# DLRM tower on one core: an unrolled, time-ordered rewriting with eleven one-hot lookups

## The chip, the cores and the metric

The kernel runs on one core of one Trainium2 chip. The metric is device time in microseconds of one execution, the median of the runs shown. TensorE (PE), VectorE (DVE), ScalarE (ACT) and GpSimd (POOL) each run their own instruction list in order; SyncE (SP) issues DMAs. They meet only at semaphores.

## The reference

```
e = stack([tbl_t[ids[:, t]] for t in 0..25], axis=1)       # 2048 x 26 x 128
combined = concat([dense[:, None, :], e], axis=1)          # 27 features of 128 numbers
inter = einsum('bfd,bgd->bfg', combined, combined)         # 27 x 27 per sample
z = concat([dense, inter[:, upper triangle]], axis=1)      # 128 + 351
h = relu(concat([z, dense]) @ W_top1 + b_top1)             # 607 -> 512
h = relu(h @ W_top2 + b_top2)                              # 512 -> 256
y = h @ W_top3                                             # 256 -> 1
```

Batch is 2048, everything float32. Twelve of the tables have 1000 rows, six 1250, seven 12500 and one 125000.

## The kernel before

The batch is cut in four blocks of 512 samples, each of four tiles of 128. The first three blocks run in a hardware loop (`Fori`), the last is written out once more. An embedding reaches PE's working tensor `emb` in one of two ways.

**Gathered** (17 tables). POOL issues one indirect DMA per table and tile (`gather`, L396), 272 in all, each fetching 128 rows. PE transposes them (`embed`, L416), and ACT copies the bank to `emb` (L535). `rows` has room for four tiles, so POOL runs a whole block ahead.

**Looked up** (9 of the 1000-row tables). The table is loaded anew for every block, ACT rounds it to float32r (`table_h`, L543), DVE subtracts to get the remainder (`table_l`, L640). DVE makes one-hot matrices: a `tensor_scalar` per 125-row chunk compares the ids, broadcast over partitions, with a per-partition row number, both operands in SBUF (L650). PE multiplies, two matmuls of 512 columns per chunk (L436, L438), 16 per lookup, and ACT copies the result to `emb` (L549, L558).

`emb` is laid out sample by sample: the 27 features of a sample lie side by side. A **gram** step (L454) is 64 small products, 26 x 26, one per sample; four samples' results go to four 32-partition strips of one PSUM bank. Each product shows as two weight loads and two matmuls in the trace. DVE copies each gram bank to SBUF (L663), turns 32 x 32 blocks (L670), and ACT and DVE collect the pairs row by row (L565, L677). PE transposes the pairs (L467), ACT and DVE split them in two parts (L574, L687), and the MLP runs in three matmuls per product: `layer1` (L485 to L488), `layer2` (L498 to L501), `layer3` (L511). ACT writes relu twice, once to SBUF in float32 (L586) and once as float32r (L588), and DVE takes the difference (L699).

The order on every engine comes from two written lists: `BODY` (grams of the block, embeds of its last two tiles, the first lookups of the next block) and `TAIL` (MLP of the block, mixed with the other lookups and first embeds of the next one). Grams stand mostly back to back in `BODY`. The PSUM banks are three for embeddings, three for grams and transposed pairs, two for the MLP.

Of the kernel before, what the change touches and what calls it, by code (L numbers as in the profile page):

```python
# [12 lines left out]
LOOKUPS = 9  # L33
LOOKED_UP = [t for t in range(TABLES) if VOCAB[t] == 1000][:LOOKUPS]
GATHERED = [t for t in range(TABLES) if t not in LOOKED_UP]

ORDER = [0] + [t + 1 for t in GATHERED] + [t + 1 for t in LOOKED_UP]


def pair_rows():  # L40

    rows = []
    for r in range(FEATURES):
        for s in range(r + 1, FEATURES):
            a, b = sorted((ORDER[r], ORDER[s]))
            rows.append(DIM + a * FEATURES - a * (a + 1) // 2 + (b - a - 1))
    return rows


def dlrm_tower(nc, dense, ids_gathered, ids_looked_up, tables, w1_dense, w1_pairs, b1, w2, b2, w3,  # L50
               out):
    fp32, fp32r = mybir.dt.float32, mybir.dt.float32r
    i32, u32 = mybir.dt.int32, mybir.dt.uint32
    ALU, ACT = mybir.AluOpType, mybir.ActivationFunctionType

    TILE, TILES = 128, 4
# [12 lines left out]
    KCH = [128, 128, PAIRS - 256, DIM]
    N1, N2 = HIDDEN1 // 128, HIDDEN2 // 128  # L70
    ONE_HOTS = 9
    assert LOOKUPS * CHUNKS % ONE_HOTS == 0

    EARLY = 2
    lookups = [("lookup", i, h) for i in range(LOOKUPS) for h in range(2)]  # L80
    early, halves = lookups[:2 * EARLY], lookups[2 * EARLY:]
    embeds = [("embed", t, e) for t in range(TILES - 2) for e in range(len(EMBED))]

    PARTS = ((3,), (0,), (1, 2))
    LAST = len(PARTS) - 1
    own = [[("layer1", 0, 0)], [("layer1", 1, 0), ("z", 0, 0), ("z", 1, 0), ("z", 2, 0)],
           [("z", 0, 1), ("z", 1, 1)], [("z", 2, 1)],
           [("layer1", 0, 1)], [("layer1", 1, 1)], [("layer1", 0, 2)], [("layer1", 1, 2)],
           [("layer1", 2, p) for p in range(3)], [("layer1", 3, p) for p in range(3)], "E",
           [("layer2", 0)], [("layer2", 1)], "E", [("layer3",)], "E", "E", "E", "E", "E", "E"]  # L90
    TAIL = [("place", i) for i in range(EARLY)] + [("pair", 1)] + halves[:1]
    spaces = own.count("E")
    for k, steps in enumerate(own):
        if steps == "E":
            n = len(embeds) // spaces
            spaces, steps, embeds = spaces - 1, embeds[:n], embeds[n:]
        TAIL += steps

        upto = -(-(k + 1) * len(halves) // len(own))
        if "E" in own[k + 1:k + 2]:  # L100
            upto += upto % 2
        TAIL += [s for s in halves[:upto] if s not in TAIL]
    assert len(TAIL) == len(set(TAIL))
    tile2, tile3 = ([("embed", t, e) for e in range(len(EMBED))] for t in (2, 3))
    BODY = [("gram", 0), ("gram", 1), ("gram", 2), *tile2, ("gram", 3), ("gram", 4),
            *early, *tile3[:-1], ("dense",), ("gram", 5, 0), tile3[-1], ("gram", 5, 1),
            ("split", EARLY + 1), ("pair", 0), ("gram", 6), ("gram", 7)]

    EMB_USES = [s for s in TAIL + BODY if s[0] == "embed" or (s in halves and s[2] == 1)]
    MIX_USES = [("gram", n) for n in range(GRAMS)] + [("z", 0), ("z", 1), ("z", 2)] + [("none",)]

    MLP_USES = [("place", i) for i in range(EARLY)] + [("layer1", n) for n in range(N1)] + \
        [("layer2", n) for n in range(N2)] + [("layer3",), ("none",)]
    assert len(MLP_USES) % 2 == 0
    assert len(EMB_USES) % 3 == 0 and len(MIX_USES) % 3 == 0

    PAIR_TILES = [slice(0, TILES - 1), slice(TILES - 1, TILES)]
    PAIR_ACT = 11
    first_pair = [r * SIDE - r * (r - 1) // 2 for r in range(SIDE)]

    ctx = ExitStack()
    with ctx:
# [9 lines left out]
        emb = sb("emb", [128, BLOCK, FEATURES])  # L136


        shared_at = nc.sbuf_base
        shared = sb("shared", [128, 2 * N1 * BLOCK])  # L140
        gram = nc.alloc_sbuf_tensor_at("gram", [128, SIDE, 128], fp32, offset=shared_at)
        h1h = nc.alloc_sbuf_tensor_at("h1h", [128, N1, BLOCK], fp32r, offset=shared_at)
        h1l = nc.alloc_sbuf_tensor_at("h1l", [128, N1, BLOCK], fp32r, offset=shared_at + N1 * BLOCK * 4)
        rows = sb("rows", [128, TILES, NG, DIM])
        dense_rows = sb("dense_rows", [128, TILES, DIM])


        shared_z_at = nc.sbuf_base
        shared_z = sb("shared_z", [128, TILES * SIDE * 32])
        turned = nc.alloc_sbuf_tensor_at("turned", [128, TILES, SIDE, 32], u32, offset=shared_z_at)  # L150
        zh = nc.alloc_sbuf_tensor_at("zh", [128, 3, BLOCK], fp32r, offset=shared_z_at)
        zl = nc.alloc_sbuf_tensor_at("zl", [128, 3, BLOCK], fp32r, offset=shared_z_at + 3 * BLOCK * 4)
        dense_h = sb("dense_h", [128, BLOCK], fp32r)
        dense_l = sb("dense_l", [128, BLOCK], fp32r)
        pairs = sb("pairs", [128, 4, PAIRS])
        gather_ids = sb("gather_ids", [128, TILES, NG], i32)
        w1h = sb("w1h", [128, 4, HIDDEN1], fp32r)
# [30 lines left out]
        zeroed = sem("zeroed")
# [581 lines left out]
```

## Time and profile before

| | |
|---|---|
| median of 3 runs | 431.82 us (426.78 to 437.46) |
| profiled execution, span | 432.4 us |
| PE / weight loads busy | 330.4 / 266.8 us |
| DVE busy | 239.1 us |
| ACT busy | 179.4 us |
| POOL busy | 308.9 us |
| mean granted TensorE clock | 0.881 |
| DMA | 49.51 MB, 115 GB/s |

The profiled execution is one more execution, with its own span; the runs are others. POOL's busy time is the issuing of gathers. Matmul records overlap their neighbours, so the sum of a group's durations is more than the engine's time on it; the distance between two starts is the rate.

### The profile page before, as it was taken

Reading aid. Unit: us, or ns where it says so; the run is one execution under the profiler, and the core shown is the slowest. Engines: PE = TensorE matmul, PEld = TensorE weight load, DVE = VectorE, ACT = ScalarE, POOL = GpSimd, SP = SyncE. Lnnn points to the kernel's source line nnn. Section 1 sums busy time; section 2 is a strip of 40 time slices with the busy share of each in tenths; the row PEclk is TensorE's granted clock in tenths of the full one; section 3 lists DMA queues with packets and bytes.
Section 4 is the critical chain, followed back from the end, with each engine's and each line's share of the span. In section 5 each row is a group of like instructions: output and inputs, shape, how many; then the busy total and the mean of one; then the engine's idle time right before and its main releaser. Section 6 shows DMA issues by size and latency. Waiting matters only on the chain.

```text
span 432.4 us, 13310 instructions
## 1 busy us (share of the span) xinstructions
PE 330.4 (76%) x5360; PEld 266.8 (62%) x5360; DVE 239.1 (55%) x471; ACT 179.4 (41%) x363; POOL 308.9 (71%) x280
## 2 busy tenths in 40 slices
PE   0785719677699998286879999376969999867596
PEld 0563517466578876275668877264758887656475
DVE  2776625397569563266768664075666758023531
ACT  2144223720746546220546545420564546323442
POOL 6887878887778877777778878777777877772000
PEclk9899977888979999659969999666879999986699
DMA  5467853435435345426444543526354442221000
GB/s 155 153 177 191 239 167 109 128 92 151 115 110 149 118 122 117 133 52 167 119 130 114 158 116 106 141 55 169 77 172 100 142 123 71 55 57 28 5 0 0
DMA packets 24707, 49.51 MB, mean 115 GB/s; under 512 B 8010, under 2 KB 10586, under 8 KB 24653
## 3 DMA queue, kind: packets, MB, share of 16 engines
q1 hardware_dynamic: 15916, 30.83, 22.4%
q0 software_dynamic: 8704, 17.84, 17.5%
q8 instruction: 47, 0.77, 0.7%
q14 instruction: 8, 0.06, 0.0%
q10 hardware_dynamic: 32, 0.01, 0.0%
HBM read 48.65 MB, written 0.01 MB: 113 GB/s over the span
## 4 chain that ended last, share of the span: by engine, by line
PE 65%; issue 15%; DMA 10%; ACT 5%; DVE 3%; SPq 0%; ACTq 0%; DVEq 0%
PE mix_ps L454 12%; PE emb_ps L436 12%; PE emb_ps L438 11%; PE emb_ps L416 6%; DMA lookup_ids<-ids_looked_up 5%; DMA table<-table 5%; PE mlp_ps L485 4%; PE mlp_ps L488 4%; PE mlp_ps L486 4%; PE mlp_ps L436 3%; PE mlp_ps L438 3%; DVE one_hot L650 2%; ACT emb L535 2%; PE mlp_ps L498 2%; PE mlp_ps L501 2%
## 5 line engine op out<-in xcount | busy, mean ns | idle before, releaser
L396 POOL DMA_INDIRECT rows<-table,gather_ids x272 | 307.9, 1132 | 83.6 <-issue 81.7
L650 DVE TENSOR_SCALAR one_hot<-lookup_ids,row_number 125x512 fp32r<-125x512 int32 x288 | 124.8, 490 | 43.6 <-DMA lookup_ids<-ids_looked_up 17.6
L436 PE MATMUL emb_ps<-one_hot,table_h 125*128 125x512 f32 x224 | 94.2, 421 | 19.1 <-DVE table_l L640 18.7
L454 PE MATMUL mix_ps<-emb 128*26 128x26 f32 x4096 | 57.7, 202 | 54.3 <-issue 51.5
L438 PE MATMUL emb_ps<-one_hot,table_l 125*128 125x512 f32 x224 | 91.9, 410 | 0.0
L454 PEld LDWEIGHTS mix_ps<-emb 128*26 128x26 f32 x4096 | 49.5, 115 | 63.6 <-issue 61.7
L543 ACT ACTIVATE table_h<-table 125x1024 fp32r<-125x1024 f32 x36 | 38.0, 1060 | 88.9 <-DMA table<-table 52.4
L535 ACT ACTIVATE emb<-emb_ps 128x512 f32<-128x512 f32 (+1 forms) x80 | 46.9, 651 | 56.5 <-PE emb_ps L416 53.2
L663 DVE COPY gram<-mix_ps 128x416 f32<-128x416 f32 x32 | 27.8, 874 | 74.3 <-PE mix_ps L454 74.1
L436 PEld LDWEIGHTS emb_ps<-one_hot,table_h 125*128 125x128 f32 x224 | 44.6, 199 | 31.7 <-ACT emb L535 12.1
L549 ACT ACTIVATE emb<-emb_ps 128x512 f32<-128x512 f32 x28 | 34.0, 1215 | 50.2 <-PE emb_ps L438 50.1
L640 DVE TENSOR_TENSOR table_l<-table,table_h 125x1024 fp32r<-125x1024 f32 x36 | 43.6, 1212 | 13.6 <-ACT table_h L543 13.6
L438 PEld LDWEIGHTS emb_ps<-one_hot,table_l 125*128 125x128 f32 x224 | 44.7, 200 | 9.2
L436 PE MATMUL mlp_ps<-one_hot,table_h 125*128 125x512 f32 x64 | 31.0, 484 | 20.2 <-DVE one_hot L650 17.5
L416 PE MATMUL emb_ps<-ident,rows 128*128 128x128 f32 x272 | 42.7, 302 | 1.9 <-ACT emb L549 1.7
L416 PEld LDWEIGHTS emb_ps<-ident,rows 128*128 128x128 f32 x272 | 36.0, 158 | 6.9 <-ACT emb L549 1.9
L436 PEld LDWEIGHTS mlp_ps<-one_hot,table_h 125*128 125x128 f32 x64 | 15.0, 235 | 26.0 <-issue 15.0
L438 PE MATMUL mlp_ps<-one_hot,table_l 125*128 125x512 f32 x64 | 29.8, 466 | 0.0
L565 ACT ACTIVATE pairs<-turned 128x24 f32<-128x24 f32 (+33 forms) x148 | 19.0, 219 | 11.7 <-DVE turned L670 11.7
L699 DVE TENSOR_TENSOR h1l<-h_full,h1h 128x512 fp32r<-128x512 f32 x16 | 11.2, 700 | 22.0 <-ACT h1h L588 22.0
L586 ACT ACTIVATE h_full<-mlp_ps,b_sb 128x512 f32<-128x512 f32 x16 | 11.0, 689 | 20.7 <-PE mlp_ps L488 20.6
L485 PE MATMUL mlp_ps<-zh,w1h 128*128 128x512 f32 (+1 forms) x48 | 19.1, 398 | 0.5 <-ACT zh L574 0.5
(50 smaller groups left out, 278.4 us busy)
## 6 DMA issues: line engine op xcount, KB each, us to landing
table<-table SPq DMA_DIRECT2D x36, 500.0 KB
lookup_ids<-ids_looked_up SPq DMA_DIRECT2D x36, 256.0 KB, 5.4
rows<-table,gather_ids POOLq DMA_INDIRECT x272, 3.9
dense_rows<-dense SPq DMA_DIRECT2D x4, 256.0 KB, 4.1
gram<-w_pairs SPq DMA_DIRECT2D x2, 256.0 KB
gram<-w_dense SPq DMA_DIRECT2D x2, 256.0 KB
h_full<-w SPq DMA_DIRECT2D x1, 512.0 KB
gather_ids<-ids_gathered SPq DMA_DIRECT2D x16, 8.5 KB, 10.2
```

The costliest lines, as they stand in the source:

```text
L396: pool.indirect_dma_start(out=rows[:, t, g, :], out_offset=None, in_=tables[GATHERED[g]], in_offset=bass.IndirectOffsetOnAxis(ap=gather_id ...
L416: last = pe.transpose(bank[:, 128 * k:128 * k + 128], src, ident[:, :])
L436: pe.matmul(bank[:, :], table_h[0:TROWS, i % 2, cols], hot, start=(c == 0), stop=False)
L438: last = pe.matmul(bank[:, :], table_l[0:TROWS, i % 2, cols], hot, start=False, stop=(c == CHUNKS - 1))
L454: last = pe.matmul(bank[32 * j:32 * j + SIDE, SIDE * q:SIDE * q + SIDE], emb[:, s, 1:FEATURES], emb[:, s, 0:SIDE], start=True, stop=True)
L485: pe.matmul(mlp_bank(("layer1", n))[:, :], w1h[0:k, c, cols], high, start=(c == 3), stop=False)
L535: act.activation(emb[:, t * TILE:(t + 1) * TILE, EMBED[e][0]:EMBED[e][0] + k], emb_bank(("embed", t, e))[:, 0:128 * k].rearrange("p (k s) ...
L543: act.activation(table_h[0:TROWS, i % 2, :], table[0:TROWS, i % 2, :], ACT.Copy) \
L549: act.activation(emb[:, :, ROWED + i], emb_bank(("lookup", i, 1))[:, :], ACT.Copy) \
L640: dve.tensor_tensor(table_l[0:TROWS, i % 2, :], table[0:TROWS, i % 2, :], table_h[0:TROWS, i % 2, :].bitcast(fp32), ALU.subtract) \
L650: dve.tensor_scalar(one_hot[0:TROWS, hot_slot(i, c), :], lookup_ids[0:TROWS, i % 2, :], row_number[0:TROWS, c:c + 1], None, ALU.is_equal) \
L663: dve.tensor_copy(gram[:, :, HALF * n:HALF * n + HALF].rearrange("p r q -> p q r"), mix_bank(("gram", n))[:, 0:SIDE * HALF].rearrange("p ( ...
```

## The change

The kernel is written anew. There are no loops: every step has a time in units of a block, the steps are sorted by it once, and all engines walk that one list. What differs:

- Eleven tables are looked up and 15 gathered (240 gathers). `rows` holds two tiles instead of four, and a gather waits for the embed step two tiles back.
- Tables are padded to 1024 rows and split by ACT and DVE in the first two blocks only. In the second the split tables are also written to a DRAM scratch (1 MB each, 11 of them), and blocks three and four load them from there, without a split. Ids are int16.
- A one-hot step is a `tensor_tensor` over two chunks, 1024 elements per partition: ids in SBUF against row numbers in a PSUM bank, each operand repeated by a zero step. There are 176 instead of 288, and room for one lookup's.
- `emb` is laid out feature by feature. The copies that fill it write whole runs of 128; the gram matmuls read their 26 columns, as weights and as moving data, at a step of 128 elements.
- ACT, not DVE, copies the gram banks, two banks for them instead of three. Pairs are collected for two tiles at a time in ten ACT copies of bands.
- The MLP and the transposed pairs share two banks. Its first relu stays in PSUM and DVE subtracts from there. The last block's MLP is done as two units of two tiles.
- Each gram is two halves in the list, and a lookup half usually stands between.

```diff
-LOOKUPS = 9
+LOOKUPS = 11
...
+    def look_time(k, h):
+        b, i = divmod(k, LOOKUPS)
+        return b - 1 + (i + h / 2 + (0.3 if b > 0 else 0.0)) / LOOKUPS
+
+    for k in range(LOOKS):
+        at(look_time(k - 3, 1) if k >= 3 else -2.0 + k / 10, "load", k)
+        if k < SPLIT_BLOCKS * LOOKUPS:
+            at(look_time(k - 1, 0) - 0.001 if k >= 1 else -1.5, "split", k)
+        if SPLIT_BLOCKS - 1 == k // LOOKUPS and SPLIT_BLOCKS < BLOCKS:
+            at(look_time(k, 0) - 0.002, "spill", k)
+        for h in range(2):
+            at(look_time(k - 1, h) + 0.001 if k >= 1 else -1.4 + h / 10, "hots", k, h)
+            at(look_time(k, h), "look", k, h)
+    for t in range(TILES):
...
+        for e in range(EMBEDS):
+            at((t + 0.02 + 0.06 * e) / PER_BLOCK if t > 0 else (-0.6, -0.5, -0.4, -0.3)[e], "embed", t, e)
+        for n in (2 * t, 2 * t + 1):
+            for h in range(2):
+                at((t + 0.4 + 0.3 * (n % 2) + 0.14 * h) / PER_BLOCK, "gram", n, h)
...
-        emb = sb("emb", [128, BLOCK, FEATURES])
+        emb = sb("emb", [128, PLACES * WIDE - 1, TILE])
...
+            def load(k):
...
+                    sp.dma_start(table_hl[:, s, :, :].bitcast(fp32), scratch[i]).then_inc(hl_in[s], 16)
+                wait(sp, hot_ready, QUADS * (k - LIDS + 1))
...
+            def spill(k):
+                sp.wait_ge(table_low, k + 1)
+                sp.dma_start(scratch[k % LOOKUPS], table_hl[:, k % HL, :, :].bitcast(fp32)).then_inc(spilled[k % HL], 16)
...
+            for t in range(TILES):
...
+                for e in range(EMBEDS):
+                    wait(pool, embeds_done, EMBEDS * (t - ROWS) + e + 1)
...
-                        last = pe.matmul(bank[32 * j:32 * j + SIDE, SIDE * q:SIDE * q + SIDE],
-                                         emb[:, s, 1:FEATURES], emb[:, s, 0:SIDE], start=True, stop=True)
+                        last = pe.matmul(bank[32 * j:32 * j + SIDE, SIDE * q:SIDE * q + SIDE],
+                                         emb[:, f + 1:f + FEATURES, s], emb[:, f:f + SIDE, s], start=True, stop=True)
...
+                act.activation(gram_sb[:, t % 2, :, HALF * side:HALF * side + HALF].rearrange("p r q -> p q r"),
+                               mix_ps[n % 2][:, 0:SIDE * HALF].rearrange("p (q r) -> p q r", r=SIDE), ACT.Copy) \
+                    .then_inc(gram_out, 1)
...
-                    dve.tensor_scalar(one_hot[0:TROWS, hot_slot(i, c), :], lookup_ids[0:TROWS, i % 2, :],
-                                      row_number[0:TROWS, c:c + 1], None, ALU.is_equal) \
-                        .then_inc(hot_ready, 1)
+                for p in (2 * h, 2 * h + 1):
+                    wait(dve, hot_used, QUADS * (k - 1) + p + 1)
+                    dve.tensor_tensor(hot[:, p, :, :],
+                                      bass.AP(lids, k % LIDS * BLOCK, [[LIDS * BLOCK, 128], [0, 2], [1, BLOCK]]),
+                                      bass.AP(row_ps, 2 * p, [[CHUNKS, 128], [1, 2], [0, BLOCK]]),
+                                      ALU.is_equal).then_inc(hot_ready, 1)
```

## Rows read from the trace of the kernel before

**Rows 1.** The page, parts 1 and 4: busy time, and the chain that ended last.

```profile
PE 330.4 (76%) x5360; PEld 266.8 (62%) x5360; DVE 239.1 (55%) x471; ACT 179.4 (41%) x363; POOL 308.9 (71%) x280
PE 65%; issue 15%; DMA 10%; ACT 5%; DVE 3%; SPq 0%; ACTq 0%; DVEq 0%
```

**Rows 2.** The page, part 5: gathers; count, busy, mean ns, idle and its releaser.

```profile
L396 POOL DMA_INDIRECT rows<-table,gather_ids x272 | 307.9, 1132 | 83.6 <-issue 81.7
```

**Rows 3.** Windows of one loop turn: busy us of each engine, clock, DMA share.

```profile
171.60:270.80 99.20, 80.02 (x1340) 65.58 (x1340) 58.17 (x116) 43.75 (x91) 77.86 (x71) 0.88 0.45 123
```

**Rows 4.** Timeline, POOL beside DVE: start us, us, instruction, idle before it.

```profile
55.76 0.94 POOL L396 DMA_INDIRECT rows<-table,gather_ids  x1 [0.30 <-issue]
...
130.09 1.88 DVE L687 TENSOR_TENSOR zl<-mix_ps,zh 128x512 fp32r<-128x512 f32 x3 [1.48 <-ACT zh L574]
...
131.16 0.94 POOL L396 DMA_INDIRECT rows<-table,gather_ids  x1 [0.30 <-issue]
...
133.47 1.21 DVE L640 TENSOR_TENSOR table_l<-table,table_h 125x1024 fp32r<-125x1024 f32 x1
134.61 1.66 DVE L650 TENSOR_SCALAR one_hot<-lookup_ids,row_number 125x512 fp32r<-125x512 int32 x4
...
133.98 2.41 POOL L396 DMA_INDIRECT rows<-table,gather_ids  x1 [0.30 <-issue]
```

**Rows 5.** Timeline, PE at the full clock: first and last of 16 lookup matmuls; transposes.

```profile
155.51 0.40 PE L436 MATMUL emb_ps<-one_hot,table_h 125*128 125x512 f32 x1
...
158.94 0.39 PE L438 MATMUL emb_ps<-one_hot,table_l 125*128 125x512 f32 x1
...
54.42 1.04 PE L416 MATMUL emb_ps<-ident,rows 128*128 128x128 f32 x8
```

**Rows 6.** Timeline, PE in grams: one at the low clock, then the last ones.

```profile
179.76 2.03 PE L454 MATMUL mix_ps<-emb 128*26 128x26 f32 x127 [2.48 <-issue]
...
399.08 1.28 PE L454 MATMUL mix_ps<-emb 128*26 128x26 f32 x128 [0.42 <-issue]
402.90 1.28 PE L454 MATMUL mix_ps<-emb 128*26 128x26 f32 x128 [2.55 <-issue]
406.36 0.49 PE L454 MATMUL mix_ps<-emb 128*26 128x26 f32 x23 [2.17 <-issue]
```

**Rows 7.** The page, part 3: DMA queues, packets, MB, share of 16 engines.

```profile
q1 hardware_dynamic: 15916, 30.83, 22.4%
q0 software_dynamic: 8704, 17.84, 17.5%
q8 instruction: 47, 0.77, 0.7%
```

**Rows 8.** Groups by line, DVE and ACT: count, busy, mean ns, idle.

```profile
L650 DVE TENSOR_SCALAR one_hot<-lookup_ids,row_number 125x512 fp32r<-125x512 int32 x288 | 124.8, 490 | 43.6 <-DMA lookup_ids<-ids_looked_up 17.6 <-PE emb_ps L438 17.2 <-PE mlp_ps L438 8.6
L535 ACT ACTIVATE emb<-emb_ps 128x512 f32<-128x512 f32 (+1 forms) x80 | 46.9, 651 | 56.5 <-PE emb_ps L416 53.2 <-ACT y_rows L600 1.7 <-issue 1.4
L549 ACT ACTIVATE emb<-emb_ps 128x512 f32<-128x512 f32 x28 | 34.0, 1215 | 50.2 <-PE emb_ps L438 50.1
L588 ACT ACTIVATE h1h<-mlp_ps,b_sb 128x512 fp32r<-128x512 f32 x16 | 10.9, 681 | 0.0
L670 DVE STREAM_TRANSPOSE turned<-gram 128x832 uint32<-128x832 uint32 x16 | 16.7, 1045 | 0.5
```

**Rows 9.** Windows: the stretch in which the DMA engines are full.

```profile
40.00:50.00 10.00, 5.24 (x25) 3.84 (x23) 6.72 (x14) 3.87 (x5) 7.87 (x8) 1.00 1.00 263
```

**Rows 10.** Timeline: the first split and the last instruction.

```profile
10.08 1.22 DVE L640 TENSOR_TENSOR table_l<-table,table_h 125x1024 fp32r<-125x1024 f32 x1 [7.01 <-ACT table_h L543]
...
430.37 0.54 ACTq L604 DMA_DIRECT2D y<-y_rows  x1
```

More of the change, by code:

```diff
@@ L67, in dlrm_tower @@
+    WIDE = 14
+    PLACE = [1, 2, 3, 4, 5, 6, 7, 8, 1, 2, 3, 9, 4, 5, 6, 7]
+    PLACES = 10
     HALF = 16
-    GRAMS = TILE // 4 // HALF * TILES
     KCH = [128, 128, PAIRS - 256, DIM]
     N1, N2 = HIDDEN1 // 128, HIDDEN2 // 128
[L71 to L82, printed above, removed]
@@ L92, in dlrm_tower @@
[L92 to L104, printed above, removed]
@@ L105, in dlrm_tower @@
[L105 to L123, printed above, removed]
+    SPLIT_BLOCKS = 2
+    HL, RAW, LIDS, ROWS = 3, 3, 2, 2
+    LOOKS = BLOCKS * LOOKUPS
+    UNITS = [(0, 4), (4, 4), (8, 4), (12, 2), (14, 2)]
+    def unit_of(tile):
+        return [u for u, (t0, n) in enumerate(UNITS) if t0 <= tile < t0 + n][0]
@@ new lines, in features, with places @@
+        def features(tile):
+            return WIDE * (PLACES - 1 - PLACE[tile])
+        def places(b, f):
+            tiles = range(b * PER_BLOCK, (b + 1) * PER_BLOCK)
+            even = all(PLACE[t] == PLACE[t - 1] + 1 for t in tiles[1:])
+            for run in ([tiles] if even else [tiles[:-1], tiles[-1:]]):
+                first = (features(run[0]) + f) * TILE
+                pitch = (PLACES * WIDE - 1) * TILE
+                yield (slice((run[0] - tiles[0]) * TILE, (run[-1] + 1 - tiles[0]) * TILE),
+                       bass.AP(emb, first, [[pitch, 128], [-WIDE * TILE, len(run)], [1, TILE]]))
@@ L442, in grams @@
-            def grams(b, n, part=None):
-                if n % 2 == 0:
-                    need = [u for u in EMB_USES if u[0] == "lookup" or u[1] == n // 2]
-                    pe.wait_ge(emb_copied, emb_no(b, need[-1]) + 1)
-                if part != 1:
-                    pe.wait_ge(*mix_before(b, ("gram", n)))
-                bank = mix_bank(("gram", n))
-                for q in (range(HALF) if part is None else range(HALF)[part * HALF // 2:][:HALF // 2]):
+                    wait_emb_bank(pe, use)
@@ L742 @@
+            dve.tensor_copy(row_ps[:, :], row_number_i[:, :]).then_inc(rows_numbered, 1)
+            dve.wait_ge(rows_numbered, 1)
+            run({"split": split, "hots": hots, "embed": embed, "gram": gram, "z": z, "l1": l1, "weights": weights})
 def kernel(**inputs):
```

894 lines of the change are left out of this document (445 added, 449 removed).

## The prediction, made before the change was run

> **What bounds the kernel now.** I read busy times and the chain first. PE is busy for 76% of the span and makes up most of the chain, with 15% of it "issue"; POOL is busy for 71% [rows 1]. That points at PE, but the share is misleading. POOL's 272 gathers take 307.9 us busy and 83.6 us idle, of which 81.7 us is its own issuing: 391.5 us without a real wait, one gather per 1.44 us [rows 2]. One loop turn lasts 99.2 us and holds 68 gathers; 68 x 1.44 = 98 us, while PE is busy for 80 of the 99 [rows 3]. So POOL paces the loop, from 2.7 us to about 396, and 36 us of last block follow.
>
> A gather isn't slow by itself. With DVE idle it is 0.94 + 0.30 = 1.24 us. Beside DVE's subtraction from a PSUM bank it is the same 0.94. Under the split of a table (two SBUF inputs) and the one-hots (`tensor_scalar`, all in SBUF) one took 2.41 [rows 4]. Of the 391.5 us, 272 x 1.24 = 337 are gathers and 54 are DVE in their way.
>
> PE is close behind. A loop turn needs nine lookups of 16 x 0.229 = 3.66 us, 72 MLP matmuls at the same 0.23 us (16.6 us), and 84 transposes at 0.13 us (11 us) [rows 5]: 61 us. Then come eight grams. A gram's 128 matmuls run in 1.28 us at the full clock, but the next one starts 3.8 us after, with 2.55 us of "issue" between them [rows 6]. 256 instructions of 64 bytes are 16 KB, and the instruction queue brought 0.77 MB in 47 pieces, 16 KB each [rows 7]. I take it that grams back to back outrun the fetching of their instructions, one piece per 3.5 to 3.9 us: 8 x 3.9 = 31 us, in all 92 us per turn against POOL's 98.
>
> **The change, part by part.**
>
> *POOL.* 240 gathers x 1.24 = 298 us. The one-hots now have one input in PSUM, which is the form that left gathers alone [rows 4]. The 22 splits remain; the one under which a gather took 2.41 cost at most 1.5 us, so 0 to 33 us, taken 13. Per tile that is 18.7 us, and `rows` lets POOL start a tile when PE embeds the one two before. If PE needs 20 us or more per tile, as below, POOL waits for PE. It stops being the pace.
>
> *DVE.* A one-hot step is 1024 elements with two tensor inputs. The nearest row is the split, also 1024 elements and two inputs: 1.21 us, the next instruction starting 1.14 after it [rows 4]. Four per lookup are 4.6 us, where eight took 3.3 (1.66 us per four). With int16, the zero steps and PSUM unseen, bounds are 0.53 us (two elements per cycle, from the 512-element step at about 0.4) and 2.2 (the strided price below); I take 1.14, since the PSUM subtraction costs 1.88 / 3 = 0.63 us for 512, the same rate. A split adds 1.14.
>
> *PE.* 11 x 3.66 = 40.3 us of lookups per block, not 33. Embeds, 16 transposes per tile, are 2.1 us on PE but 4 x 0.65 = 2.6 on ACT, which empties the banks [rows 8]; 10 us per block. Since grams are halved with a lookup half (1.8 us) between, most of the fetching hides: 1.3 us at the full clock plus 0.5 for the quarter of them still adjacent, 1.8 us, 14.4 per block. Bounds are 1.3 and 3.9.
>
> *The layout of `emb`.* Nothing here shows PE reading at a step. ACT writes at one: 512 elements take 1.215 us against 0.681 [rows 8], an extra of 1.0 ns per element, and at most 2.4 ns in all. For 26 columns that is 27 to 62 ns per record, against 10 ns from start to start today. But four strips run side by side: at 1.2 GHz, with a column per cycle [rows 5], 26 columns would be 21.7 ns, and starts are 2.03 / 127 = 16 ns apart [rows 6]. Spread over four strips, 27 to 62 becomes 7 to 16, so 1.3 to 2.0 us per gram. I take no charge beyond the 1.8.
> The Trainium skill ("Advanced Engine Details and Errata", SBUF Cachelines) says that accesses which each touch another 16-byte line pay a penalty. The ACT row agrees; the page gives no price for PE. By this rule without the strips' overlap the result would be the slow rival below.
>
> *DMA.* In the second block each lookup moves 0.5 MB of table, 1.0 of spill, 0.13 of ids and 5.5 gathers (0.36 MB). The SP queue moved 30.83 MB in 22.4% of the span, 318 GB/s, the gathers 236 [rows 7]: 5.1 + 1.5 = 6.6 us per lookup, 73 per block, plus 1.8 MB of weights, 79. By the full stretch at 263 GB/s [rows 9] it is 90. Later blocks need 1.49 MB, 5.1 us per lookup, under PE's time.
>
> *ACT.* It gains 32 gram copies (0.7 to 1.0 us) and loses strides; about 200 us by the durations of its rows, no pace anywhere.
>
> **The sum**, by the stages of the list:
> 1. First block's lookups, nothing else for PE to do. DVE starts its first split at 10.1 [rows 10]; 11 x 5 x 1.14 = 62.7; PE's last half and the copy 2.5: 75 us.
> 2. Second block's lookups, grams of the first: PE 40 + 10 + 14 = 65, DVE 62.7 + 4 turns (4.2 [rows 8]) + weights 5 = 73, DMA 79 to 90: 80.
> 3. and 4. PE 40.3 + 16.6 + 1.6 + 0.6 + 10 + 14.4 = 84 each; DVE 50 + 10.
> 5. The last block without lookups. Grams lie bare again but for the MLP: up to the last gram three tile pairs of about 9 (compute 2.6 + 5.6), embeds 4 x 2.6, pairs 2.3, first small unit 6, last grams 8: 54. Then copy, turn, ten pair copies (3), z 2, 12 x 4 matmuls of 256 columns 6, relus 1.5, layer 2 3, layer 3 and the store 4: 21. Before, from the last gram (406.4) to the end it was 26 with 512 columns [rows 6, 10]. 75.
>
> 75 + 80 + 84 + 84 + 75 = 398, and 0.1 us per lookup for hand-overs: **402 us** against the profiled execution's 432.4, which is as good as the median, 431.82.
>
> **The rivals.**
> - *Strided reads are not hidden (slower).* Weights and moving columns at a step of 512 bytes, one strip at a time: 27 to 62 ns per record are 3.5 to 7.9 us per gram. In stages 3 and 4 all of it beyond 1.8 is added, in stage 2 what passes the 15 us that PE has free, in stage 5 what passes 3.9. At 45 ns (5.8 us): 64 + 17 + 15, so 498 us; 429 at 27 ns. It makes the kernel over 2% slower from 32 ns (4.1 us per gram). For it: ACT's price, and both reads are strided. Against: the overlap of strips [rows 6].
> - *The engines wait for one another.* One lookup's worth of one-hots, two tiles of `rows`, two MLP banks also for the pairs, written orders with DMAs of 1 MB ahead of the ids on one queue. If stages 2 to 4 each reach 90 to 95 and the first 80: 420 to 445, centre 430, no change. For it: ids were waited for 17.6 us before [rows 8]. Against: DVE has 24 us free per block in stages 3 and 4.
> - *Better than the sum.* Fetching wholly hidden (8 x 0.5 per stage), DMA at its queue rate, the last stage at 65: 375 to 388.
> - *The gathers keep colliding.* At 1.44 us a tile would take 21.6 us, PE's own 21; at most 8 us more, inside the forecast's own range.
>
> **How the numbers follow.** Forecast 0.46 (388 to 420), waits 0.26 (418 to 445), strided 0.16 (429 to 566), better 0.12. The range 375 to 450 leaves out half of the better case's tail and three quarters of the strided one. This kernel's runs spread over 2.5%, so under 2% can't be told from no change. Faster by over 2% (under 423): 0.46 + 0.12 + 0.04 of the waits = 0.62. Within 2%: 0.15, waits. Slower: 0.07 + 0.16 = 0.23.
>
> **What would show it.** Gathers at 0.94 and 0.30 us under one-hots, and waits for PE's embeds in their row; if the mean stays near 1.13 the POOL step is wrong. One-hot steps 1.14 us apart. Grams' 64 records in about 0.65 us; at over 2 us the layout is the loss. Grams of the first tile from about 80 us on; DMA share near 0.9 from 80 to 160, then lower; PE over 0.9 busy from 160 to 325 at a clock near 1; and the last 20 us a chain from ACT to PE and back. PE waiting on `hot` or on loads in the middle stages would be the second rival.

## The result, and the profile after

The kernel after takes 465.5 us (median of 4 runs, 464.0 to 466.7), the kernel before 430.8 in the same session (4 runs). The ratio is 1.082, 95% interval [1.073, 1.090]: slower, where 402 us and faster were forecast. The profiled execution has a span of 463.8 us. Some executions of a kernel are 1.5% or more above its fastest; two of the four of hot_scalar (632 and 633 us) and one of the four of w_early (656 us) are such ones, and the times given for these two below leave them out.

The page of the kernel after: busy times, the chain by engine and by line, and the costliest groups (same columns as in [rows 1, 2, 8]).

```profile
PE 406.9 (88%) x5528; PEld 326.6 (70%) x5528; DVE 326.0 (70%) x276; ACT 213.5 (46%) x362; POOL 253.4 (55%) x247
...
PE 48%; DVE 37%; issue 6%; ACT 5%; DMA 2%; SPq 1%; ACTq 0%; DVEq 0%
...
L380 POOL DMA_INDIRECT rows<-table,gather_ids x240 | 252.6, 1053 | 155.5 <-PE emb_ps L416 84.0 <-issue 70.1 <-DMA gather_ids<-ids_gathered 1.4
L622 DVE TENSOR_TENSOR hot<-lids,row_ps 128x1024 fp32r<-128x1024 int16 x176 | 250.1, 1481 | 9.9 <-PE emb_ps L402 9.8
...
L432 PE MATMUL mix_ps<-emb 128*26 128x26 f32 x4096 | 109.3, 285 | 2.7 <-ACT emb L527 2.6
```

POOL was 71% busy and never waited for PE [rows 1, 2]; now it waits 84 us for PE's embeds. PE went from 330 to 407 us busy. The rest is read by stages, cut at the first gram of each block. First the kernel before in these cuts, then the kernel after. "Stage" is the forecast's word: 1 ends at the first gram of block 1, 5 begins at the first gram of block 4. Columns: stretch, its us, then busy us (and records) of PE, PEld, DVE, ACT, POOL, granted clock, DMA share, GB/s.

```profile
0.00:78.80 78.80, 44.78 (x180) 34.39 (x180) 42.26 (x86) 24.96 (x28) 61.79 (x59) 0.91 0.59 171
78.80:176.70 97.90, 79.95 (x1342) 65.03 (x1341) 61.68 (x118) 48.04 (x96) 77.51 (x67) 0.91 0.43 123
176.70:275.90 99.20, 80.02 (x1340) 65.56 (x1340) 58.17 (x116) 43.77 (x90) 77.87 (x71) 0.88 0.44 122
275.90:373.60 97.70, 83.33 (x1343) 67.26 (x1344) 58.89 (x116) 41.54 (x88) 76.68 (x70) 0.85 0.39 108
373.60:432.40 58.80, 42.34 (x1161) 34.51 (x1160) 18.06 (x35) 21.03 (x65) 15.05 (x16) 0.85 0.08 22
```

```profile
0.00:76.00 76.00, 56.42 (x208) 35.88 (x208) 70.86 (x67) 22.67 (x31) 51.30 (x52) 1.00 0.55 164
76.00:180.30 104.30, 85.80 (x1280) 67.42 (x1279) 93.82 (x74) 49.13 (x81) 61.26 (x53) 0.92 0.73 247
180.30:278.90 98.60, 96.48 (x1369) 79.54 (x1370) 75.70 (x59) 45.45 (x88) 57.57 (x60) 1.00 0.55 179
278.90:375.20 96.30, 93.02 (x1349) 76.38 (x1348) 68.40 (x52) 45.65 (x76) 56.87 (x58) 1.00 0.44 141
375.20:463.80 88.60, 75.23 (x1333) 67.42 (x1332) 17.25 (x27) 50.62 (x86) 26.42 (x27) 0.94 0.08 22
```

Stage 1 is as forecast (76.0 against 75). In stages 3 and 4 PE is busy for 96.48 of 98.6 and 93.02 of 96.3: it is the pace, as forecast, but each takes 12 to 15 us more than the 84 given to it. Against the kernel before, the stages 2 to 4 took 97.9, 99.2 and 97.7 us and now take 104.3, 98.6 and 96.3; the last block, written as two units with bare grams, went from 58.8 to 88.6.

Timeline of the kernel after, all engines, around one whole gram (start, us, instruction).

```profile
209.14 3.19 PE L432 MATMUL mix_ps<-emb 128*26 128x26 f32 x128
...
209.25 2.90 ACT L512 ACTIVATE emb<-emb_ps 128x384 f32<-128x384 f32 x2 [0.61 <-PE emb_ps L402]
209.95 6.28 DVE L622 TENSOR_TENSOR hot<-lids,row_ps 128x1024 fp32r<-128x1024 int16 x4
210.22 0.94 POOL L380 DMA_INDIRECT rows<-table,gather_ids  x1 [0.30 <-issue]
```

A gram's 128 records take 3.19 us; before they took 1.28 at the full clock [rows 6]. And something else happens: two ACT copies, of 0.49 us each where no gram runs, begin with the gram and are done 2.90 us later, 0.2 us before its end, and four one-hot steps take 6.28 us instead of 4.61. All durations of these two lines in the kernel after (count: min/median/max in ns):

```profile
L622 DVE TENSOR_TENSOR hot<-lids,row_ps x176: 1150/1214/3733, 7.8 to 365.3; 128x1024 fp32r<-128x1024 int16 x176
...
L512 ACT ACTIVATE emb<-emb_ps x55: 265/598/3335, 14.9 to 369.4; 128x512 f32<-128x512 f32 x33, 128x384 f32<-128x384 f32 x11, 128x128 f32<-128x128 f32 x11
```

In the second stage DVE and PE stand still for some 9 us, behind the MLP's weights. Timelines of the kernel after, DVE, then PE; then two windows of 4 us, in the stage's columns:

```profile
88.71 0.69 DVE L660 TENSOR_TENSOR w_stage<-w_stage 128x512 f32<-128x512 f32 x1 [9.13 <-DMA b_sb<-b]
...
89.98 2.35 DVE L622 TENSOR_TENSOR hot<-lids,row_ps 128x1024 fp32r<-128x1024 int16 x2
...
91.25 0.80 PE L400 MATMUL emb_ps<-hot,table_hl 128*128 128x512 f32 x1 [8.75 <-DVE hot L622]
...
84.00:88.00 4.00, 0.00 (x0) 0.00 (x0) 0.00 (x0) 0.00 (x0) 0.00 (x0) 0.59 0.95 305
88.00:92.00 4.00, 0.75 (x2) 0.66 (x3) 3.29 (x4) 2.83 (x4) 0.00 (x0) 0.50 0.03 9
```

The DMA engines are full while the two wait (share 0.95), and idle just behind it (0.03).

### The profile page after: what moved, and what is told of

It reads as the page before. It is cut to its first block, busy times and chain, and to the rows that moved or that the text cites. A ratio compares the mean times of both kernels' runs of the same rounds, so it can differ in the third digit from the quotient of the medians.

```text
span 463.8 us, 12402 instructions
## 1 busy us (share of the span) xinstructions
PE 406.9 (88%) x5528; PEld 326.6 (70%) x5528; DVE 326.0 (70%) x276; ACT 213.5 (46%) x362; POOL 253.4 (55%) x247
## 4 chain that ended last, share of the span: by engine, by line
PE 48%; DVE 37%; issue 6%; ACT 5%; DMA 2%; SPq 1%; ACTq 0%; DVEq 0%
DVE hot L622 27%; PE mix_ps L432 14%; PE emb_ps L400 8%; PE emb_ps L402 7%; DVE table_hl L614 5%; PE mlp_ps L465 4%; PE mlp_ps L467 3%; PE mlp_ps L466 3%; PE emb_ps L416 2%; PE mlp_ps L476 2%; PE mlp_ps L478 2%; PE mlp_ps L477 2%; DVE turned L643 1%; DMA b_sb<-b 1%; ACT pairs L549 1%
## 5 line engine op out<-in xcount | busy, mean ns | idle before, releaser
L380 POOL DMA_INDIRECT rows<-table,gather_ids x240 | 252.6, 1053 | 155.5 <-PE emb_ps L416 84.0
L622 DVE TENSOR_TENSOR hot<-lids,row_ps 128x1024 fp32r<-128x1024 int16 x176 | 250.1, 1481 | 9.9 <-PE emb_ps L402 9.8
L400 PE MATMUL emb_ps<-hot,table_hl 128*128 128x512 f32 x352 | 152.7, 434 | 36.4 <-DVE hot L622 34.1
L402 PE MATMUL emb_ps<-hot,table_hl 128*128 128x512 f32 x352 | 141.8, 403 | 0.0
L432 PEld LDWEIGHTS mix_ps<-emb 128*26 128x26 f32 x4096 | 102.9, 214 | 21.3 <-issue 17.4
L400 PEld LDWEIGHTS emb_ps<-hot,table_hl 128*128 128x128 f32 x352 | 67.8, 193 | 69.9 <-DVE hot L622 23.5
L432 PE MATMUL mix_ps<-emb 128*26 128x26 f32 x4096 | 109.3, 285 | 2.7 <-ACT emb L527 2.6
L512 ACT ACTIVATE emb<-emb_ps 128x512 f32<-128x512 f32 (+2 forms) x55 | 55.2, 1041 | 89.8 <-PE emb_ps L402 89.8
L402 PEld LDWEIGHTS emb_ps<-hot,table_hl 128*128 128x128 f32 x352 | 68.3, 194 | 11.1
L537 ACT ACTIVATE gram_sb<-mix_ps 128x416 f32<-128x416 f32 x32 | 30.3, 948 | 31.8 <-PE mix_ps L432 31.7
L614 DVE TENSOR_TENSOR table_hl<-raw,table_hl 128x1024 fp32r<-128x1024 f32 x22 | 28.1, 1276 | 4.1 <-ACT table_hl L503 4.1
L503 ACT ACTIVATE table_hl<-raw 128x1024 fp32r<-128x1024 f32 x22 | 24.9, 1131 | 6.8 <-DMA raw<-table 6.8
```

What stands on the lines that cost most here:

```text
L380: pool.indirect_dma_start(out=rows[:, t % ROWS, g, :], out_offset=None, in_=tables[GATHERED[g]], in_offset=bass.IndirectOffsetOnAxis(ap=ga ...
L400: pe.matmul(bank[:, :], table_hl[:, k % HL, 0, cols], hot[:, p, c % 2, :], start=(c == 0), stop=False)
L402: last = pe.matmul(bank[:, :], table_hl[:, k % HL, 1, cols], hot[:, p, c % 2, :], start=False, stop=(c == CHUNKS - 1))
L432: last = pe.matmul(bank[32 * j:32 * j + SIDE, SIDE * q:SIDE * q + SIDE], emb[:, f + 1:f + FEATURES, s], emb[:, f:f + SIDE, s], start=True, ...
L512: last = act.activation(here, emb_bank(use)[:, samples].rearrange("p (t s) -> p t s", s=TILE), ACT.Copy)
L537: act.activation(gram_sb[:, t % 2, :, HALF * side:HALF * side + HALF].rearrange("p r q -> p q r"), mix_ps[n % 2][:, 0:SIDE * HALF].rearran ...
```

## The experiments

My theory after the result: the gram's reads of `emb` at a step of 512 bytes are the loss, on both operands. Rivals: the stretched writes of ACT and DVE, the PSUM form of the one-hots, the weight loads, the gram copies on ACT.

The runs fell on two kinds of chip, and this matters: where the result above was taken, and on the chip of layout_again, gram_dve and layout_early_scalar, the kernel before takes about 431 us, on four others 705 to 708. Every ratio is to the kernel before on the same chip. I give "431 us chip" or "705 us chip" with each.

**The kernel after again (705 us chip).** No edit.

> The changed kernel as it is, on the chip of its neighbours here, since four variants ran on a chip on which the kernel before took 705 us instead of 431 and TensorE stood 150 us on 'issue'. If that chip's instruction fetching was the cause, this chip either repeats it (then this run is the base for those four as well: about 690 us) or doesn't (465 us).

655.9 us, ratio 0.930 [0.924, 0.937]. The kernel that is 8% slower on one chip is 7% faster here. Timeline of it, PE, and PE's largest wait:

```profile
150.18 1.11 PE L432 MATMUL mix_ps<-emb 128*26 128x26 f32 x37
151.69 0.34 PE L432 MATMUL mix_ps<-emb 128*26 128x26 f32 x5 [0.40 <-issue]
152.45 0.33 PE L432 MATMUL mix_ps<-emb 128*26 128x26 f32 x4 [0.42 <-issue]
153.20 0.32 PE L432 MATMUL mix_ps<-emb 128*26 128x26 f32 x4 [0.43 <-issue]
...
PE mix_ps L432 <- issue: 139.9, 159, 1.9
```

Within grams PE gets one to five records per 0.7 us, in stretches of some 15 us, and stands idle for nothing else that the trace shows, 139.9 us in all. On the 431 us chip the same line is idle for 2.7 us. I take it that on these chips PE lacks instructions, and not data; that is inferred, since "issue" only says that the trace shows nothing that PE waited for. It isn't all of the 190 us: PE is also busy for 459.5 us instead of 406.9, at a mean granted clock of 0.83 instead of 0.97. The kernel before wasn't profiled there; why it loses more (274 us against 190) stays open.

**Which side of the gram is slow (705 us chips).** Other numbers of `emb` are read, so these three compute something else; only the addresses' steps differ.

```
-  emb[:, f + 1:f + FEATURES, s],       emb[:, f:f + SIDE, s]
+  emb[:, f + 1 + s % SIDE, 0:SIDE],    emb[:, f + s % SIDE, 0:SIDE]    # g_both
+  emb[:, f + 1 + s % SIDE, 0:SIDE],    emb[:, f:f + SIDE, s]           # g_weights
+  emb[:, f + 1:f + FEATURES, s],       emb[:, f + s % SIDE, 0:SIDE]    # g_moving
```

Naming: `g_weights` and `g_moving` make that operand contiguous and leave the other at the step.

> The changed kernel, but each gram product reads 26 neighbouring numbers of one feature, as weights and as moving data, where it read one number of each of 26 features; so the grams are of other numbers and the output isn't the reference's. Same instructions, counts and order. Theory S (the step of 128 elements is the loss: a gram half takes 1.74 us where 0.65 was expected, and writes to SBUF by ScalarE and VectorE that overlap it last until it ends): a gram half takes 0.65 to 0.85 us, the longest one-hot step falls from 3.7 to under 1.6 us, ScalarE's copies to under 0.75, and the time falls from 465 to 385 to 405 us. Rival D (VectorE's one-hots of two tensors pace the kernel, the chain has 27% of them; grams fill time that TensorE would wait anyway): the grams shorten, but the time stays above 440 us. Rival Q (waits from the written order, the two-tile row buffer and the queue of loads): above 440 us as well, with longer waits of TensorE for one-hots.

> The changed kernel, with only the weights of a gram product read from 26 neighbouring numbers, the moving data still at the step of 128 elements (the output isn't the reference's). Theory S in the form 'each read costs by itself': half of the gain of both, 420 to 440 us, and the stretched writes stay in part. If the moving read sets the 25.6 ns per record, the gram half stays at 1.7 us and the time at 455 to 466; if the weights do, it is as with both. Rival D: no change, 460 to 468.

> The changed kernel, with only the moving data of a gram product read from 26 neighbouring numbers, the weights still at the step of 128 elements (the output isn't the reference's). Theory S, each read by itself: 420 to 440 us. If the moving read is the slow one, a gram half falls under 0.9 us and the time to 385 to 405; if the weights are, 455 to 466. Rival D: no change, 460 to 468.

Ratios 0.870 [0.864, 0.875], 0.894 [0.888, 0.900], 0.897 [0.891, 0.902]. Both single ones were run again on another chip, the first on a third as well, to see whether a 431 us chip shows the same; none was met. In the expectation of the repeats I had the two operands' names crossed. Nothing hangs on it, as they agree: 0.890 [0.882, 0.898] and 0.886 [0.881, 0.890] for the one, 0.894 [0.886, 0.902] for the other.

> The kernel after in which the grams read their weights at the step of 512 bytes and their moving columns side by side (which of the embedding's numbers a gram reads changes, so it computes other numbers). Theory: half a gram takes 1.1 to 1.2 us instead of 1.74, and no write of ACT or DVE to SBUF is stretched under it (one-hot steps at most 1.3 us, L512 at most 0.7 for 512 elements): 425 to 435 us on a chip of 431 us, and within 3 us of the kernel with the moving columns alone at a step. Rival (each side has its own price and stretches writes by its own share): one-hot steps of 2 us and more under grams, 440 us or more.

> The kernel after in which the grams read their moving columns at the step of 512 bytes and their weights side by side (other numbers). Theory: as with the weights alone at a step, 1.1 to 1.2 us per half gram, no stretched writes, 425 to 435 us on a chip of 431 us. Rival (only one of the two sides, the weights, is slow): half a gram at 0.7 us and 415 us or less.

Timelines of g_weights on its third chip and of g_moving on its second, half a gram (64 records); under each all one-hot steps, and under the first all L512 copies (min/median/max):

```profile
85.35 1.18 PE L432 MATMUL mix_ps<-emb 128*26 128x26 f32 x64
...
L622 DVE TENSOR_TENSOR hot<-lids,row_ps x176: 1181/1215/1233, 7.1 to 500.3; 128x1024 fp32r<-128x1024 int16 x176
L512 ACT ACTIVATE emb<-emb_ps x55: 268/597/674, 15.3 to 506.5; 128x512 f32<-128x512 f32 x33, 128x384 f32<-128x384 f32 x11, 128x128 f32<-128x128 f32 x11
```

```profile
86.76 1.20 PE L432 MATMUL mix_ps<-emb 128*26 128x26 f32 x64
...
L622 DVE TENSOR_TENSOR hot<-lids,row_ps x176: 1181/1212/1232, 7.1 to 502.0; 128x1024 fp32r<-128x1024 int16 x176
```

Half a gram takes 0.73 us with neither side at the step, 1.18 to 1.20 with one, 1.74 with both. Each side costs about 0.5 us per 64 records (7 to 8 ns per record), and they add. All these grams run on four strips, so whether the strips hide a part of the price isn't shown. The stretching needs both sides: with one, the longest one-hot step in any of the five traces is 1.24 us instead of 3.7, the longest L512 0.69 instead of 3.3.

The Trainium skill's rule ("Advanced Engine Details and Errata", SBUF Cachelines: accesses that each touch another 16-byte line pay) agrees: for PE by these times, and for ACT, whose L512 copies have a median of 0.60 us in the kernel after and of 1.07 where they write at the step (trace of layout_again, below). The Trainium skill's page "SBUF — State Buffer" (Who interferes with whom) says that ACT waits for nobody; here ACT copies of 0.6 us took up to 3.3 under grams with both operands at the step, so for this pattern the measurement decides against it.

**The layout undone (both kinds).** All else is as in the kernel after. The copies of the lookups to `emb`, not shown, write at the step as well.

```
-  emb = sb("emb", [128, PLACES * WIDE - 1, TILE])
+  emb = sb("emb", [128, TILE, PLACES * WIDE - 1])
...
-  emb[:, f + 1:f + FEATURES, s], emb[:, f:f + SIDE, s]
+  emb[:, s, f + 1:f + FEATURES], emb[:, s, f:f + SIDE]
...
-  act.activation(emb[:, f + WIDE + 4 * e:f + WIDE + 4 * e + 4, :], bank[:, :].rearrange("p (k s) -> p k s", k=4), ACT.Copy)
+  act.activation(emb[:, :, f + WIDE + 4 * e:f + WIDE + 4 * e + 4], bank[:, :].rearrange("p (k s) -> p s k", k=4), ACT.Copy)
```

> The changed kernel with one part undone: emb is laid out sample by sample again (a row of all features per sample, 139 numbers), so the grams read 26 neighbouring numbers on both sides and ScalarE writes at a step. Complete and with the reference's output. Theory S: a gram half 0.65 to 0.75 us instead of 1.74, no one-hot step over 1.3 us, ScalarE's lookup copies 1.2 us instead of 0.6 but hidden; 32 grams x 1.8 us and some of VectorE's 49 us of stretching go, and 465 becomes 390 to 410 us, faster than the kernel before by 5 to 9%. Rival D (one-hots pace it): 440 us or more. Rival A (ScalarE's stepped writes, 44 x 0.6 us dearer, come on the path instead): 420 to 440.

> The kernel after with emb back in the order sample by sample (both reads of a gram at a step of 4 bytes, the copies that fill it write at the step). Theory: against the kernel after it gains 1.0 us per half gram on PE and the time that ACT and DVE were held up under grams, some 40 to 60 us. On a chip on which the kernel before takes 431 us, the kernel after takes 465, so 405 to 425 us, a ratio of 0.94 to 0.99; on a chip of 705 us it repeats 612 us, 0.868. Rival (the 8% were another step's, and the layout's gain only shows where instructions come slowly): on a 431 us chip the ratio stays at 1.05 or above.

On a 705 us chip 612.5 us, 0.868 [0.863, 0.873]: the same as g_both, so the copies that now write at the step cost nothing that shows there. On a 431 us chip 419.4 us (417.8 to 421.8), 0.974 [0.966, 0.982]. That is 46 us less than the kernel after. Layout undone, 431 us chip: groups, all one-hot steps, all L512 copies, half a gram, and the stages in the same cuts.

```profile
L380 POOL DMA_INDIRECT rows<-table,gather_ids x240 | 236.5, 985 | 137.8 <-issue 70.1 <-PE emb_ps L416 66.4 <-DMA gather_ids<-ids_gathered 1.4
L622 DVE TENSOR_TENSOR hot<-lids,row_ps 128x1024 fp32r<-128x1024 int16 x176 | 203.8, 1210 | 20.9 <-PE emb_ps L402 14.4 <-DMA lids<-ids_looked_up 6.4
L432 PE MATMUL mix_ps<-emb 128*26 128x26 f32 x4096 | 52.2, 192 | 8.4 <-issue 4.6 <-ACT emb L527 2.8
...
L622 DVE TENSOR_TENSOR hot<-lids,row_ps x176: 1181/1210/1224, 7.3 to 330.8; 128x1024 fp32r<-128x1024 int16 x176
L512 ACT ACTIVATE emb<-emb_ps x55: 422/1068/1126, 15.3 to 335.5; 128x512 f32<-128x512 f32 x33, 128x384 f32<-128x384 f32 x11, 128x128 f32<-128x128 f32 x11
...
126.42 0.73 PE L432 MATMUL mix_ps<-emb 128*26 128x26 f32 x64
...
0.00:75.50 75.50, 56.56 (x208) 36.91 (x208) 70.84 (x67) 27.37 (x31) 50.89 (x52) 1.00 0.53 165
75.50:171.50 96.00, 72.31 (x1277) 54.73 (x1276) 75.09 (x74) 45.43 (x81) 53.47 (x55) 0.88 0.79 269
171.50:257.30 85.80, 82.32 (x1367) 64.49 (x1366) 59.78 (x59) 40.74 (x88) 51.83 (x56) 1.00 0.62 203
257.30:342.60 85.30, 80.31 (x1350) 62.95 (x1350) 51.70 (x51) 40.15 (x76) 55.94 (x60) 0.98 0.51 160
342.60:415.80 73.20, 59.52 (x1333) 51.28 (x1332) 14.87 (x27) 36.23 (x87) 25.19 (x27) 0.95 0.11 27
```

Stages 3, 4 and 5 are 85.8, 85.3 and 73.2 us where 84, 84 and 75 were forecast. Only stage 2 isn't: 96 against 80. There DVE waits 10.12 us for the same DMA, and PE 10.8 us in one wait for one-hots.

**The weight loads apart.** The nine loads of the MLP's weights stand together on SP's queue at the start of stage 2 (76.2 to 82.6 us in the kernel after), ahead of the next table load. They become seven pieces between the table loads of the first block, in stage 1. The expectation of the three edits together, below, says "of the second block"; the kernel that ran issues them in the first.

```
+    for j in range(7):
+        at(look_time(j, 1) + 0.002, "piece", j)
...
-  if j > 0: return
-  sp.dma_start(w1_stage[:, 0, :], w1_pairs[0:128, :]).then_inc(weights_in, 16)
-  ...
+  def piece(j):
+      if j == 0:
+          sp.dma_start(w1_stage[:, 0, :], w1_pairs[0:128, :]).then_inc(weights_in, 16)
+      ...
```

> The changed kernel with one part moved: the nine loads of MLP weights are issued one or a few per lookup during the first block, and not all behind lookup 11, where the ids of the next lookup stood behind them and VectorE waited 9 us. Theory W (that wait is on the path): 9 to 10 us less, 455 us. Rival: the loads now delay tables and ids of the first block, which is paced by VectorE at 5.7 us a lookup; then the first gram comes later than 76 us and the gain is 0 to 5 us.

> Both: emb sample by sample, and the weights' loads spread over the first block. Complete, with the reference's output. Theories S and W together: the two gains add, 380 to 400 us, against the kernel before faster by 7 to 12%. If without the dear grams the second block is paced by DMA (1.6 MB per lookup), W gains less here than alone, and it stays within 5 us of the layout alone.

Alone 647.3 us, 0.917 [0.911, 0.923], 8.6 us better than the kernel after; with the layout undone 602.7, 0.857 [0.850, 0.864], 10 us better than the layout alone. Two more chips, also of 705 us, gave 0.852 [0.845, 0.859] and 0.851 [0.848, 0.855]. By the first grams of the blocks all of the 10 us are in stage 2: it takes 119.9 us instead of 129.7, and stage 1 ends at 84.3 us in both traces. The edit does two things at once: the wait for the weights is gone, and their 1.8 MB leave stage 2, where the DMA engines were full during that wait. Which of the two counts wasn't tried. With the layout undone and nothing else changed it was not met on a 431 us chip.

**One-hots as `tensor_scalar`.** Two of 512 elements with the row number as a scalar from SBUF take the place of one `tensor_tensor` of 1024 against PSUM.

```
-  row_ps = ctx.enter_context(nc.psum_tensor("row_ps", [128, CHUNKS], fp32))
+  row_ps = sb("row_f", [128, CHUNKS])
...
-  dve.tensor_tensor(hot[:, p, :, :], bass.AP(lids, ...), bass.AP(row_ps, 2 * p, [[CHUNKS, 128], [1, 2], [0, BLOCK]]), ALU.is_equal)
+  for c in range(2):
+      last = dve.tensor_scalar(hot[:, p, c, :], lids[:, k % LIDS, :], row_ps[:, 2 * p + c:2 * p + c + 1], None, ALU.is_equal)
```

> The changed kernel, with the one-hots made as before: two tensor_scalar instructions of 512 elements with the row number in SBUF in place of one tensor_tensor of 1024 against the PSUM bank. Theory S: VectorE does a lookup's one-hots in 3.3 us instead of 4.6, which shortens the first stage from 76 to 62 to 66 us, and little else, since TensorE is busy from 180 us on: 448 to 460 us; gathers take 1.2 us or more again under them. Rival D: one-hots pace it throughout, so 44 x 1.3 = 57 us go: 405 to 415 us. Rival Q: no change.

> The kernel after with emb sample by sample and one-hots as two tensor_scalar of 512 elements, row numbers in SBUF; weight loads as in the kernel after. Layout, one-hots and early loads together gave 389.2 us, layout alone 419.4. Theory: DVE paces the first block at 11 x 5 x 1.14 = 62.7 us; at 3.3 + 1.14 per lookup it is 49, so the first block gets 12 to 14 us shorter and the second little (weight loads, DMA): 402 to 408 us, 0.93 to 0.95. Rival (the gathers get in the way: 1.16 us instead of 0.98 each, 240 of them): under 6 us of gain, 413 or more.

Alone 618.0 and 618.7 us where the kernel before takes 705.0, a quotient of 0.877 (two runs, so no interval), against 0.930 for the kernel after: 37 us, where 5 to 17 were expected. With the layout undone 597.4, 0.844 [0.836, 0.852], against 0.868 for the layout alone. By the first grams of the blocks stage 1 gets 22 us shorter in both cases (61.2 against 83.5, 62.0 against 84.3). With the layout undone stage 2 gives 6 of them back; alone, stage 3 is another 19 us shorter, and why isn't shown. Trace of hot_scalar, its gathers:

```profile
L380 POOL DMA_INDIRECT rows<-table,gather_ids x240 | 306.2, 1276 | 233.8 <-PE emb_ps L416 162.8 <-issue 69.5 <-DMA gather_ids<-ids_gathered 1.5
```

The gathers do get slower, 1276 ns on average instead of 985 to 1053, and it doesn't matter: POOL waits for PE 163 us anyway.

**The gram copies back on DVE (431 us chip).**

```
-  act.activation(gram_sb[:, t % 2, ...], mix_ps[n % 2][:, 0:SIDE * HALF]..., ACT.Copy).then_inc(gram_out, 1)
+  dve.tensor_copy(gram_sb[:, t % 2, ...], mix_ps[n % 2][:, 0:SIDE * HALF]...).then_inc(gram_out, 1)
```

> The kernel after with the gram banks copied by DVE again (32 copies of 0.7 to 1.0 us move from ACT to DVE). Theory: this part of the change is worth little; in the blocks where DVE makes one-hots at 4.6 us per lookup the copies add 8 x 0.9 = 7 us to it per block, in the second block that is on the path, in the others it is not, and DVE is also held up under grams: 0 to 15 us slower than the kernel after (656 us on a chip of 705: a ratio of 0.93 to 0.95; 465 on a chip of 431: 1.08 to 1.115). Rival (ACT was late with these copies and PE waited for them): 5 us or more faster than the kernel after.

474.9 us, 1.100 [1.091, 1.108], 8 to 9 us slower than the kernel after (7.7 by the ratios, 9.4 by the medians); 7.6 us of it are in stage 2, by the first grams. Its copies, min/median/max:

```profile
L638 DVE COPY gram_sb<-mix_ps x32: 852/914/2428, 96.2 to 453.2; 128x416 f32<-128x416 f32 x32
```

So this part of the change is a gain of some 8 us, as long as the rest stays.

**All three edits (431 us chip).**

> Three edits of the kernel after together: emb back sample by sample, one-hots as two tensor_scalar of 512 elements with the row numbers in SBUF (0.41 us each, 3.3 us per lookup instead of 4.6), and the MLP's weight loads put apart in seven pieces between the table loads of the second block. Theory: layout and early loads alone gave 602.7 us where the kernel before takes 705 (0.857); the faster one-hots shorten the first two blocks, where DVE is the pace, by up to 11 x 1.3 = 14 us each, less what the gathers lose to DVE's use of SBUF: 580 to 595 us, a ratio of 0.82 to 0.845. On a chip of 431 us: 375 to 400 us, 0.87 to 0.93. Rival (the gathers, which a two-input SBUF form of DVE holds up, become the pace again): no gain over 602.7 us, 0.855 or more.

389.2 us (387.1 to 392.4), 0.902 [0.894, 0.911]: faster than both kernels. Its stages and its gathers:

```profile
0.00:62.70 62.70, 50.94 (x208) 39.09 (x208) 55.71 (x116) 28.77 (x32) 51.89 (x37) 1.00 0.67 211
62.70:145.80 83.10, 69.27 (x1281) 53.79 (x1281) 59.81 (x120) 45.42 (x80) 66.64 (x55) 0.92 0.83 290
145.80:230.80 85.00, 82.49 (x1365) 64.66 (x1364) 47.66 (x104) 40.89 (x88) 65.81 (x64) 1.00 0.64 210
230.80:314.80 84.00, 80.20 (x1352) 63.35 (x1351) 40.11 (x89) 40.59 (x76) 64.99 (x63) 0.98 0.52 165
314.80:387.60 72.80, 59.12 (x1333) 50.50 (x1332) 14.80 (x27) 35.98 (x86) 29.29 (x31) 0.98 0.12 31
...
L390 POOL DMA_INDIRECT rows<-table,gather_ids x240 | 277.8, 1158 | 74.2 <-issue 72.5 <-DMA gather_ids<-ids_gathered 1.4 <-PE emb_ps L426 0.3
```

Stages 1 and 2 lose 12.8 and 12.9 us against the layout alone, the others are as they were. How the 12.9 divide between the one-hots and the weights wasn't measured on this chip. POOL now hardly waits (0.3 us for PE's embeds): gathers are again near the pace.

The kernel before itself was run as one of these kernels on this chip, too, to see its trace where it takes 705 us. The chip was a 431 us one; it took 437.0 us, so no trace shows it at 705.

> The kernel before itself, profiled on the kind of chip on which it takes 705 us instead of 431. Theory (instruction supply): here too PE gets its instructions in a trickle for stretches, about one stretch per 300 matmuls. The kernel before has 5360 matmul records against 5168 or so of the kernel after, so it should lose at least as much: PE issue over 200 us in the whole span, most of it inside the gram line, where groups of 128 records should be cut in pieces of 1 to 5 records about 0.7 us apart; gathers no longer back to back. Rival (the chip's memory is slow for it): the added time would stand behind waits for DMAs, and the gram groups would keep their 1.28 us. If the chip should be one on which it takes 431 us, the profile repeats the earlier one and the runs beside it can be read against that.

## Why the prediction was wrong

| stage | forecast | after | layout undone | all three edits |
|---|---|---|---|---|
| 1 | 75 | 76.0 | 75.5 | 62.7 |
| 2 | 80 | 104.3 | 96.0 | 83.1 |
| 3 | 84 | 98.6 | 85.8 | 85.0 |
| 4 | 84 | 96.3 | 85.3 | 84.0 |
| 5 | 75 | 88.6 | 73.2 | 72.8 |
| span | 402 | 463.8 | 415.8 | 387.6 |

**The step that failed: "The layout of `emb`", "I take no charge beyond the 1.8".** It divided the step's price by four strips, set the quotient against the time of a record instead of adding it, and counted it once for two operands. A gram took 3.2 us where 1.8 stood, and undoing the layout gives 0.5 + 8.3 + 12.8 + 11.0 + 15.4 = 48.0 of the 61.8 us missed. PE's busy time in grams fell by more, from 109.3 to 52.2 us. Part of the difference is a new wait: PE's lookups wait 9.2 us for ACT's copies, which now write at the step, where they waited 0.4. Other waits moved as well, so the account isn't closed.

The rows never gave a factor of four: 21.7 ns of columns against starts 16 ns apart is 1.36, at the low clock. At the full clock 26 columns are 26 x 0.229 / 512 = 11.6 ns against starts 10 ns apart [rows 5, 6]. And these are records of unit step, which say nothing of how long reads at a step take. That the lower bound, 27 ns per record one after another, lies near the measured 3.2 / 128 = 25 ns is luck. The 27 were ACT's 1.0 ns per element, taken once; PE pays 7 to 8 ns per record and operand, some 0.3 ns per column, twice, on top of the 11 ns (0.73 / 64) of a record at unit step.

**The strided rival** named the mechanism, but its own working gives 429 at 27 ns, 36 short. It let stage 2 absorb 15 us and let stage 5 pay only beyond 3.9 us per gram, the pitch that I had put down to instruction fetching. Stage 2 paid 8.3 and stage 5 15.4. With halved grams at 0.73 us and 4.6 us of "issue" in the gram line of the whole layout-undone trace, no such floor was left: no part of a gram's price could disappear in it. The floor of 3.9 belonged to the back-to-back grams of the kernel before.

**Stage 2** lacked a wait. The forecast counted the weights as bytes (79 us of DMA) and DVE time (5 us). It didn't ask what is queued behind the wait for them: L660 stands in DVE's list ahead of the next one-hots, and nine loads stand on SP's queue ahead of the next table. The wait costs 10.8 us of PE time with the layout undone. Taking the loads out of the stage gives 8.6 to 10 us on 705 us chips, bytes and wait together. Stage 2 of the forecast (80) is 16 us short of the layout-undone kernel, so some 6 us stay unexplained; the forecast's own upper figure for the DMA there was 90. Its sum for DVE is slightly off too: 62.7 + 4.2 + 5 is 71.9, not 73. The second rival ("engines wait for one another") was right in kind for this, though not in the ids that it named.

**The stretched instructions** were in neither the forecast nor a rival. DVE is busy for 46.3 us more with the one-hots than with the layout undone (250.1 against 203.8). PE's L400 waited 34.1 us for one-hots in the kernel after and 24.0 with the layout undone, so about 10 of the 48 us may be theirs. This isn't shown: no run has stretched instructions without slow grams.

**What held.** POOL stopped being the pace: gathers at a median of 947 ns and 84 us of waits for PE. One-hot steps: 1.21 us long, four in 4.61, as taken. Stages 1, 3, 4, 5 within 2 us once the layout is undone. They hold as sums, and partly by luck: the grams' 14.4 us in them are 16 x 0.73 = 11.7. But the PSUM form of the one-hots, whose point in my sum was to leave gathers alone, is a net loss, 15 us or more on 705 us chips (612.5 against 597.4 with the layout undone, on two chips): 4.6 instead of 3.3 us per lookup where DVE paces, to spare gathers that wait for PE in any case.

**Against the kernel before** the stages add up to -2.8 + 6.4 - 0.6 - 1.4 + 29.8 = +31.4 us, nearly all in the last block. 15.4 of that are the slow grams; the other 14.4 were in the forecast, which allowed 16.2 (75 against 58.8).

## What to carry to other kernels

Price an operand at a step per record and per operand, and add the two to the record's own time; overlap seen on records of unit step is no reason to divide the price, until a row shows records at a step overlapping. Where small transfers are placed in a list, count their bytes and then read, on each engine's list, what stands behind the instruction that waits for the last of them. And before a cost is hidden under another engine's or the fetcher's floor, check that this floor still exists in the new order of work.

## What the runs showed of the hardware

- 26-column f32 matmul records, reading SBUF at a step of 512 bytes: 64 in 0.73 us with no operand at the step, 1.18 and 1.20 with one (moving, weights), 1.74 with both, at the full clock.
- With both operands at the step, ACT and DVE instructions that write SBUF and overlap a gram last to about its end (0.6 to 3.3 us, 1.2 to 3.7); with one operand at the step the same two lines (L512, L622) stay at 0.69 and 1.24 or under. Which part of the memory makes them wait was not tried.
- The same two kernels compare as 1.082 on one chip and as 0.930 on another. On the slower chips PE gets, in stretches, one to five gram records per 0.7 us, and stands 120 to 157 us on "issue" in the gram line, in every variant traced there; that its instructions come too slowly is inferred. What the layout costs is nearly the same on both (46 and 43 us).
